# Six slots later: the loads of the context and of its transpose for the output side

## The chip, the cores and the metric

The kernel runs on one core of a Trainium2 chip. The metric is device time in microseconds of one launch, the median of a few runs. Engines are named as in the profile: PE is TensorE (PEld its weight loads), DVE is VectorE, ACT is ScalarE, POOL is GpSimd, SP is SyncE. SP and ACT also issue DMAs; their queues appear as SPq and ACTq.

## The reference

Two cross-attention layers over a batch of four, all in float32. Inputs are x (4, 256, 256) and a context (4, 512, 256).

```
# layer 0
q, k, v = LN(x) @ q_w + q_b, ctx @ k_w + k_b, ctx @ v_w + v_b      # 16 heads of 16
out     = softmax(q k^T / 4 + mask) v                               # 256 x 512 per head
hid     = out @ cproj_w + cproj_b + x
x1      = hid + gelu(LN(hid) @ fc_w + fc_b) @ proj_w + proj_b       # inner width 1024
# layer 1, one head of width 256
q, k, v = x1 @ w_q^T, ctx @ w_k^T, ctx @ w_v^T
result  = x1 + alpha * softmax(q k^T / 16) v @ w_o^T
```

## The kernel before

All matrix products are of float32 numbers that are split into a high and a low part (`_h`, `_l`; ScalarE makes the high part, VectorE or GpSimd the low one), three products for one.

**Slots.** Time is cut by hand into slots. A batch b has four groups of four heads, and a group has 8 slots. In slot s of group g, TensorE computes one tile of scores for the exponentials (`exp_tile`, L693, two matmuls), ScalarE takes its exponential (`exp`, L1107), and in between TensorE computes the score tiles from which VectorE takes the row maxima for the group one ahead (`max_tile`, L672; L1411), and the products with the values of the group one behind (`pv`, L703). Iteration b covers slots 7 to 38 (`at` in the code), where slots 8 to 15 belong to group 1, 16 to 23 to group 2, 24 to 31 to group 3, and 32 to 38 already to group 0 of batch b + 1. Beside the attention of batch b each slot has steps of two other batches:

- `pre(b + 1, ...)`: layer norm, transpose, query, key and value projections of the next batch (`PRE_AT` slots 9, 10, 16 and 22, `V_AT` 36 and 38).
- `post(b - 1, ...)`: the output projection, the second layer norm, the GELU layers and all of layer 1 for the batch before (`POST_AT`, or `LATE_AT` for batch 2). Of these, `NT` (slot 8 or 9) needs the rows x in `h`, `CT0` and `CT1` (slots 22 and 25, late 27 and 30) need the transposed context in `pT_raw` (L1126), and `CX` (27, late 34) needs the context in `pcx` (L1173).

Each engine runs its own program in this order; engines wait for one another by semaphores. There are two engines that issue DMAs.

**SyncE** loads the inputs of the next batch (`load_pre`), and stacks: `stack_group(b, g)` copies queries and keys of a group, high and low parts, into `q_stack` and `k_stack` (on-chip to on-chip), so that one matmul makes all three products at once. For one group these are three transfers of 64 KB (L520), a mask row (L525) and three of 128 KB (L530), the low part of the keys (`kp_l`) last. There is room for three groups, so the stacking of group 3 of a batch is released at slot 8, when the exponentials of group 0 have been computed; the groups 0 and 1 of the next batch follow at slots 16 and 24, and group 2 at slot 32. Each is read first eight slots after that. Nothing is stacked for a batch after the last.

**ScalarE** issues `load_post(b - 1)` (L1246 to L1251) at the beginning of slot `LOAD_AT` = 8 of iterations 1 to 3: the rows into `h` (256 KB), the context into `pcx` (512 KB), and its transpose into `pT_raw` (512 KB). Before the first it waits for `h_free`, the store of the batch before. The stores come from ScalarE as well (L1256).

In slot 10, `pre(b + 1, U_Q)` on ScalarE writes the high part of the next batch's queries over `qp_h` (L1079). It waits for TensorE's product and, by `await_stacked(act, range(NG), b)`, for the stacking of all four groups of the present batch, whose last transfer is the low part of the keys of group 3. GpSimd's `mask_row_of` (slot 11, L1740) waits for the same.

Of the kernel before, what the change touches and what calls it, by code (L numbers as in the profile page):

```python
# [94 lines left out]

GELU_CUBE, GELU_TANH, GELU_Y, GELU_SPLIT = 1, 2, 3, 4

LOAD_AT = 8


MAX_TILES = ((0, 1), (2, 3), (4,), (5,), (6,), (7,), (), ())
# [32 lines left out]
def build(nc, x, ctx, mask, ln1_w, ln1_b, q_w, q_b, k_w, k_b, v_w, v_b, cproj_w, cproj_b, ln2_w, ln2_b,  # L134
          fc_w, fc_b, proj_w, proj_b, l1_q, l1_k, l1_v, l1_o, alpha, ctx_t, q_t, k_t, vectors, out):
    with ExitStack() as stack:
# [177 lines left out]
        def steps_at(b):  # L314
            return LATE_AT if b == B - 2 else POST_AT

        def pre_at(b):
            return EARLY_AT if b == 1 else PRE_AT
# [150 lines left out]
        def slots(b, last):  # L469

            for at in range(START, START + NS):
                ab = b + 1 if at >= NS else b
                yield at, ab, at % NS // SLOTS, at % SLOTS, not (last and at >= NS)
# [593 lines left out]
        def _(act):  # L1067
            def pre(b, n):
                if U_K <= n < U_V:
                    return  # L1070
                act.wait_ge(pre_full, pre_use(b, n))
                if n < U_Q:

                    act.activation(zT[0][:].rearrange("p c n -> p (c n)"), pre_bank(b, n), ACT.Copy).then_inc(pre_hi, 1)
                elif n == U_Q:

                    await_stacked(act, range(NG), b)
                    for c in range(DC):
                        a = act.activation(qp[0][:, c, :], pre_bank(b, n)[:, c * LQ:(c + 1) * LQ], ACT.Identity, bias=bq[:, c:c + 1])  # L1079
                    a.then_inc(qh_done, 1)  # L1080
                elif n >= U_V:
                    i = n - U_V
                    await_(act, pv_done, NG * b)
                    act.activation(vals[:, 2 * i:2 * i + 2, :, 0:HD],
                                   pre_bank(b, n).rearrange("p (t h d) -> p t h d", t=2, h=H), ACT.Copy).then_inc(pre_free, 1)

            def context_high(b, c):

                act.wait_ge(cx_in, 16 * (b + 1))
                await_(act, pre_full, PRE_USES * b)  # L1090
                act.activation(cT[0][:, c, :], cx[:, c, :], ACT.Copy).then_inc(ct_high, 1)
# [18 lines left out]
            def o_out(b, g):  # L1110
                act.wait_ge(pv_done, NG * b + g + 1)
                act.activation(oT[:, g, :], om[:, 0:LQ], ACT.Copy).then_inc(o_done, 1)
# [51 lines left out]
            def post_slot(b, at):  # L1164

                if is_f(b, at - GELU_SPLIT):
                    gelu_high(b, chunk_of(b, at - GELU_SPLIT))
                if at in steps_at(b):
                    post(b, steps_at(b)[at])
                if steps_at(b).get(at) == "CX":  # L1170

                    wait_context(act, b)
                    act.activation(pc[0][:], pcx[:], ACT.Copy).then_inc(cx_high, 1)  # L1173
                if is_f(b, at - GELU_TANH):
                    gelu_tanh(b, chunk_of(b, at - GELU_TANH))

            def post_slot_end(b, at):
                if steps_at(b).get(at - 1) in ("S0", "S1"):
                    exp1(b, int(steps_at(b)[at - 1][1]))
# [51 lines left out]
            def tail_slot(at):  # L1231
                for i in tail_chunks(at - GELU_SPLIT):
                    tail_y_high(i)
                for step in tail_steps(at):
                    tail(step)
                for i in tail_chunks(at - GELU_TANH):
                    tail_tanh(i)
                for step in tail_steps(at - 1):
                    if step in ("S0", "S1"):
                        tail_exp(int(step[1]))  # L1240

            def pre_slot_end(b, at):
                if pre_at(b).get(at - 1, 0) >= U_K:
                    key_high(b, pre_at(b)[at - 1] - U_K)

            def load_post(b):  # L1246

                act.wait_ge(h_free, 16 * (b + 1))
                act.dma_start(h[:], x[b].rearrange("(p t) d -> p t d", t=TQ)).then_inc(h_in, 16)
                act.dma_start(pcx[:], ctx[b].rearrange("(p k) d -> p k d", k=TK)).then_inc(pcx_in, 16)  # L1250
                act.dma_start(pT_raw[:], ctx_t[b].rearrange("(c p) n -> p c n", p=P)).then_inc(pT_in, 16)  # L1251

            def store(b):
                bank, count = post_use(b, W_DL)
                act.wait_ge(post_free[bank], count + 1)
                act.dma_start(out[b].rearrange("(p t) d -> p t d", t=TQ), h[:]).then_inc(h_free, 16)  # L1256

            def prepare(step):
                if step == "WA":
                    act.wait_ge(prep_ps, 1)  # L1260
                    act.activation(wa[0][:].rearrange("p c n -> p (c n)"), work_ps[:, work_bank("prep", 0, "WA"), :], ACT.Copy, scale=L1_SCALE)\
                       .then_inc(w_hi, 1)
                elif step == "WO":
                    act.wait_ge(prep_ps, 3)
                    act.activation(wo[0][:].rearrange("p c n -> p (c n)"), work_ps[:, work_bank("prep", 0, "WO"), :], ACT.Copy).then_inc(w_hi, 1)
                elif step == "WC":
                    act.wait_ge(wc_in, 16 * NG)
                    act.activation(wc[0][:], raw_c, ACT.Copy).then_inc(w_hi, 1)
                elif step[:2] == "WF":
                    k = int(step[2])  # L1270
                    act.wait_ge(wf_in, 16)
                    act.activation(wf[0][:, k, :], raw_f[:, k, :], ACT.Copy, scale=vecs[:, V_LN2W + k:V_LN2W + k + 1])\
                       .then_inc(w_hi, 1)
                elif step[:2] == "WP":
                    half = slice(int(step[2]) * FC // 2, (int(step[2]) + 1) * FC // 2)
                    act.wait_ge(wp_in, 16)
                    act.activation(wp[0][:, half, :], raw_p[:, half, :], ACT.Copy, scale=0.5).then_inc(w_hi, 1)
# [26 lines left out]
            def attend(b, g, s):  # L1304
                nb, ng = ahead(b, g)
                pb_, pg = behind(b, g)
                if s == O_AT and not (isinstance(pb_, int) and pb_ < 0):
                    o_out(pb_, pg)
                exp(b, g, s)
                if s == ROWS_AT and not (isinstance(nb, int) and nb == B):  # L1310
                    max_rows(nb, ng)

            def iteration(b, first, last):
                for at, ab, g, s, attends in slots(b, last):
                    if not first and at == LOAD_AT:
                        load_post(b - 1)
                    if not last and at in CT_AT:
                        context_high(b + 1, CT_AT[at])
                    if not last and at in pre_at(b + 1):
                        pre(b + 1, pre_at(b + 1)[at])  # L1320
                    if not last and at in V_AT:
                        pre(b + 1, U_V + V_AT[at])
                    if not first:
                        post_slot(b - 1, at)
                    elif at in PREP_AT:
                        prepare(PREP_AT[at])
                    if last:
                        tail_slot(at)
                    if attends:
                        attend(ab, g, s)  # L1330
                    elif s == 0:
                        o_out(b, NG - 1)
                    if not last:
                        pre_slot_end(b + 1, at)
                    if not first:
                        post_slot_end(b - 1, at)
                    if not first and steps_at(b - 1).get(at - 1) == "DL":
                        store(b - 1)

            def epilogue():  # L1340
                for at in range(START + NS, LAST_SLOT):
# [3 lines left out]
                    if steps_at(B - 2).get(at - 1) == "DL":  # L1345
                        store(B - 2)

            run(act, iteration, prologue, epilogue)


# [546 lines left out]
```

## Time and profile before

| | us |
|---|---|
| median of three runs | 310.41 (308.37, 310.41, 323.36) |
| the profiled execution's own time | 313.87 |
| its span, first to last instruction | 312.1 |
| mean granted TensorE clock | 0.973 |
| TensorE busy | 268.1 (86%) |
| VectorE busy | 212.4 (68%) |
| ScalarE busy | 176.6 (57%) |
| GpSimd busy | 89.3 (29%) |
| DMA queue of SyncE (q1) | 17.31 MB, 23.8% of 16 engines |
| DMA queue of ScalarE (q10) | 5.52 MB, 6.4% |
| `k_stack<-kp_l` in the chain that ended last | 8% of the span |

Times of a row count from the first instruction of the span. Busy is the time in which an engine has an instruction running; a wait is told by its idle time and by what released it. The chain that ended last is followed back from the last instruction to whatever released each step. In this execution iteration 1 has its slot 8 at about 91.5 us, iteration 2 at 160.7 and iteration 3 at 228.4.

### The profile page before, as it was taken

To read this page: it belongs to the slowest core of one execution; us is meant where nothing else is said; L and a number is where in the kernel's file an instruction comes from. 1 tells how busy PE (TensorE), PEld (TensorE's weight loads), DVE (VectorE), ACT (ScalarE), POOL (GpSimd) and SP (SyncE) were. 2 spreads that over 40 slices of the span, in tenths; PEclk is the share of its full clock that TensorE was granted. 3 is DMA by queue.
4 is the path that set the end of the run, shared out by engine and by line. 5 is a ranking of instruction groups with operands and counts; after the bars stand their busy time and mean duration, and the time that the engine had idled before them with its cause. 6 is when DMAs were issued, how large, how long until landed. Compare 5 with 4: busy or idle time off the path is not lost.

```text
span 312.1 us, 5297 instructions
## 1 busy us (share of the span) xinstructions
PE 268.1 (86%) x2012; PEld 214.4 (69%) x2012; DVE 212.4 (68%) x368; ACT 176.6 (57%) x329; POOL 89.3 (29%) x108
## 2 busy tenths in 40 slices
PE   0757878997998699898988799998999999898995
PEld 0644647794676588676876587775877798578974
DVE  6776685677589458965488498847478766366854
ACT  3221575668472485956371786765375777526622
POOL 5551011102022139530012257430031174344100
PEclk9989599999799799999999999999999999999999
DMA  6038847711359002111638030205055000000000
GB/s 211 1 97 159 225 90 224 188 54 27 79 135 207 13 28 51 46 34 58 130 104 175 2 75 4 79 0 110 11 192 81 3 0 2 0 0 2 2 34 34
DMA packets 16456, 23.16 MB, mean 74 GB/s; under 512 B 2528, under 2 KB 9184, under 8 KB 16416
## 3 DMA queue, kind: packets, MB, share of 16 engines
q1 hardware_dynamic: 13360, 17.31, 23.8%
q10 hardware_dynamic: 3072, 5.52, 6.4%
q8 instruction: 16, 0.26, 0.4%
q14 instruction: 8, 0.07, 0.1%
HBM read 12.07 MB, written 1.05 MB: 42 GB/s over the span
## 4 chain that ended last, share of the span: by engine, by line
PE 54%; DVE 13%; DMA 8%; ACT 8%; POOL 7%; issue 5%; SPq 3%; ACTq 0%; POOLq 0%; DVEq 0%
PE work_ps L621 11%; DMA k_stack<-kp_l 8%; PE s L672 7%; PE om L703 6%; PE s L693 6%; PE work_ps L625 5%; DVE neg_max L1411 5%; PE work_ps L608 4%; ACT probs L1107 2%; PE s L621 2%; PE om L679 2%; SPq L520 2%; POOL ft L1771 2%; POOL max_cols L1727 1%; DVE ft L1480 1%
## 5 line engine op out<-in xcount | busy, mean ns | idle before, releaser
L1411 DVE TENSOR_REDUCE neg_max<-s 128x1 f32<-128x512 f32 x128 | 83.7, 684 | 20.8 <-PE s L672 20.3
L1107 ACT ACTIVATE probs<-s 128x512 f32<-128x512 f32 x128 | 75.5, 599 | 29.2 <-PE s L693 28.7
L693 PE MATMUL s<-q_stack,k_stack 128*128 128x256 f32 x256 | 57.5, 308 | 6.2 <-ACT probs L1107 5.4
L672 PE MATMUL s<-k_stack,q_stack 96*128 96x512 f32 x128 | 53.8, 453 | 4.7 <-DVE neg_max L1411 4.2
L693 PEld LDWEIGHTS s<-q_stack,k_stack 128*128 128x128 f32 x256 | 44.6, 200 | 14.0 <-ACT probs L1107 8.0
L672 PEld LDWEIGHTS s<-k_stack,q_stack 96*128 96x128 f32 x128 | 24.0, 202 | 20.9 <-DVE neg_max L1411 12.5
L703 PE MATMUL om<-probs,vals 128*17 128x256 f32 x512 | 33.7, 382 | 0.0
L1727 POOL CAST max_cols<-neg_max 128x8 fp32r<-128x8 f32 x16 | 5.8, 363 | 96.3 <-DVE neg_max L1411 96.3
L1099 ACT ACTIVATE q_stack<-om 8x1024 fp32r<-8x1024 f32 x16 | 16.3, 1018 | 8.1 <-PE om L679 7.8
L703 PEld LDWEIGHTS om<-probs,vals 128*17 128x17 f32 x512 | 11.9, 96 | 10.7 <-issue 0.3
L1422 DVE TENSOR_TENSOR y_l<-work_ps,y_h 128x512 fp32r<-128x512 f32 x12 | 8.3, 690 | 13.2 <-ACT y_h L1121 13.2
L1121 ACT ACTIVATE y_h<-work_ps 128x512 fp32r<-128x512 f32 x12 | 7.1, 596 | 17.7 <-PE work_ps L625 14.2
L1776 POOL TENSOR_TENSOR y_l<-fx,y_h 128x512 fp32r<-128x512 f32 x9 | 12.5, 1392 | 10.7 <-ACT y_h L1161 10.7
L1480 DVE SCALAR_TENSOR_TENSOR ft<-ft,fx 128x512 f32<-128x512 f32 x9 | 9.5, 1051 | 8.2 <-POOL ft L1771 8.2
L1745 POOL TENSOR_TENSOR kp_l<-kp_l,kp_h 128x512 fp32r<-128x512 f32 x7 | 9.0, 1284 | 20.7 <-ACT kp_h L1095 20.7
L1771 POOL TENSOR_TENSOR ft<-fx 128x512 f32<-128x512 f32 x9 | 10.3, 1139 | 11.1 <-ACT fx L1135 11.1
L608 PE MATMUL work_ps<-wv_h,cT_h 128*128 128x256 f32 x32 | 9.9, 309 | 3.4 <-DVE wv_l L1496 3.3
L679 PE MATMUL om<-ident,max_cols 128*104 128x128 f32 x32 | 7.1, 306 | 6.6 <-POOL max_cols L1729 6.6
L621 PE MATMUL work_ps<-aT_h,wf_h 128*128 128x256 f32 x48 | 12.7, 294 | 0.0
L621 PE MATMUL work_ps<-aT_h,wf_l 128*128 128x256 f32 x48 | 12.5, 291 | 0.0
L1079 ACT ACTIVATE qp_h<-work_ps,bq 128x256 fp32r<-128x256 f32 x8 | 3.4, 470 | 15.7 <-DMA k_stack<-kp_l 11.1
L621 PE MATMUL work_ps<-wp_h,y_h 128*128 128x256 f32 x48 | 12.0, 283 | 0.0
(290 smaller groups left out, 670.4 us busy)
## 6 DMA issues: line engine op xcount, KB each, us to landing
k_stack<-kp_h SPq DMA_DIRECT2D x32, 128.0 KB
cx<-in_ctx_t_dram SPq DMA_DIRECT2D x4, 512.0 KB, 4.5
k_stack<-kp_l SPq DMA_DIRECT2D x16, 128.0 KB
q_stack<-qp_h SPq DMA_DIRECT2D x32, 64.0 KB
pcx<-in_ctx_dram ACTq DMA_DIRECT2D x3, 512.0 KB, 4.7
pT_raw<-in_ctx_t_dram ACTq DMA_DIRECT2D x3, 512.0 KB, 9.8
xz<-in_x_dram SPq DMA_DIRECT2D x5, 256.0 KB, 4.1
q_stack<-qp_l SPq DMA_DIRECT2D x16, 64.0 KB
```

Source lines behind the costliest of these rows:

```text
L608: mm = pe.matmul(o, wi(w[a], k), vi(v[c], k), start=start and k == 0 and i == 0, stop=stop and k == n - 1 and i == 2)
L621: pe.matmul(o, wi(w[a], k), vi(v[c], k), start=start and i == k == a == c == 0, stop=False)
L625: mm = pe.matmul(o, wi(w[late[0]], k), vi(v[late[1]], k), start=False, stop=stop and i == len(terms) - 1 and k == n - 1)
L672: pe.matmul(s1[:, s1_bank(b, SLOTS * g + s), :], q_stack[0:ROW_MAX, hd, chunk(t)], k_stack[0:ROW_MAX, hd, :], start=True, stop=True).then_ ...
L679: mm = pe.transpose(om_rows[0:ROWS, chunk(t)], max_cols[:, t, :].bitcast(F32), ident[:])
L693: mm = pe.matmul(s2[:, s2_bank(b, SLOTS * g + s), i * LQ:(i + 1) * LQ], k_stack[:, hd, chunk(k)], q_stack[:, hd, :], start=True, stop=True)
L703: mm = pe.matmul(om[32 * j:32 * j + VW, 0:LQ], vals[:, k, j * NG + g, :], probs[:, g % 2, j, k, :], start=k == 0, stop=k == TK - 1)
L1099: act.activation(q_stack[ROW_MAX:ROWS, slots_of(b, g), :], om_rows[ROW_MAX:ROWS, :].unsqueeze(1).to_broadcast([2 * GH, GH, LQ]), ACT.Copy) ...
L1107: act.activation(probs[:, g % 2, s // 2, k:k + 2, :], s2[:, s2_bank(b, SLOTS * g + s), :].rearrange("p (k n) -> p k n", k=2), ACT.Exp).the ...
L1411: dve.tensor_reduce(neg_max[:, g % 2, s % 2, s // 2:s // 2 + 1], s1[:, s1_bank(b, SLOTS * g + s), :], AX.X, ALU.max, negate=True).then_inc ...
L1480: dve.scalar_tensor_tensor(f, f, 1.0 / GELU_CUBIC, fx[i % 3], ALU.add, ALU.mult).then_inc(cube, 1)
L1771: pool.tensor_tensor(ft[i % 3], fx[i % 3], fx[i % 3], ALU.mult).then_inc(square, 1)
```

## The change

`load_post` is split in two. The rows are still loaded at slot 8, behind the wait for `h_free`. The context and its transpose are issued at the beginning of slot 14, by the same engine, into the same buffers, with the same semaphores.

```
--- before.py
+++ after.py
@@ -95,7 +95,7 @@
 
 GELU_CUBE, GELU_TANH, GELU_Y, GELU_SPLIT = 1, 2, 3, 4
 
-LOAD_AT = 8
+LOAD_AT, LOAD_CONTEXT_AT = 8, 14
 
 
 MAX_TILES = ((0, 1), (2, 3), (4,), (5,), (6,), (7,), (), ())
@@ -1243,10 +1243,13 @@
                 if pre_at(b).get(at - 1, 0) >= U_K:
                     key_high(b, pre_at(b)[at - 1] - U_K)
 
-            def load_post(b):
+            def load_rows(b):
 
                 act.wait_ge(h_free, 16 * (b + 1))
                 act.dma_start(h[:], x[b].rearrange("(p t) d -> p t d", t=TQ)).then_inc(h_in, 16)
+
+            def load_context(b):
+
                 act.dma_start(pcx[:], ctx[b].rearrange("(p k) d -> p k d", k=TK)).then_inc(pcx_in, 16)
                 act.dma_start(pT_raw[:], ctx_t[b].rearrange("(c p) n -> p c n", p=P)).then_inc(pT_in, 16)
 
@@ -1313,7 +1316,9 @@
             def iteration(b, first, last):
                 for at, ab, g, s, attends in slots(b, last):
                     if not first and at == LOAD_AT:
-                        load_post(b - 1)
+                        load_rows(b - 1)
+                    if not first and at == LOAD_CONTEXT_AT:
+                        load_context(b - 1)
                     if not last and at in CT_AT:
                         context_high(b + 1, CT_AT[at])
                     if not last and at in pre_at(b + 1):
```

## Rows read from the trace of the kernel before

**Rows 1.** Window, slots 8-16: length, engines' busy us, PEclk, DMA share, GB/s.

```profile
91.55:112.09 20.54, 16.07 (x119) 12.64 (x118) 12.97 (x30) 9.98 (x20) 4.26 (x6) 0.92 0.46 94
```

**Rows 2.** The chain that ended last: start us, duration us, what.

```profile
95.41 9.08 DMA k_stack<-kp_l
...
104.59 0.84 ACT qp_h L1079 x2
...
164.56 8.07 DMA k_stack<-kp_l
...
172.74 0.85 ACT qp_h L1079 x2
...
232.25 9.24 DMA k_stack<-kp_l
```

**Rows 3.** Waits of the whole span: us, times, longest us.

```profile
ACT qp_h L1079 <- DMA k_stack<-kp_l: 11.1, 2, 6.1
```

**Rows 4.** Line L530: who waited for it (us, times).

```profile
  PEld s L672: 0.3, 1
```

**Rows 5.** TensorE's timeline: start us, us, instruction [idle before <-releaser].

```profile
100.42 0.28 PE L608 MATMUL work_ps<-zT_h,wq_l 128*128 128x256 f32 x1
...
103.04 0.50 PE L672 MATMUL s<-k_stack,q_stack 96*128 96x512 f32 x1
...
105.97 0.58 PE L693 MATMUL s<-q_stack,k_stack 128*128 128x256 f32 x1 [2.43 <-ACT probs L1107]
...
169.65 0.28 PE L608 MATMUL work_ps<-zT_h,wq_l 128*128 128x256 f32 x1
...
174.12 0.50 PE L693 MATMUL s<-q_stack,k_stack 128*128 128x256 f32 x2 [1.36 <-ACT probs L1107]
...
175.09 0.51 PE L693 MATMUL s<-q_stack,k_stack 128*128 128x256 f32 x2 [0.24 <-ACT probs L1107]
```

**Rows 6.** Windows with stacking in flight, and after it (columns as rows 1).

```profile
98.00:100.80 2.80, 2.80 (x32) 2.23 (x24) 2.48 (x9) 0.48 (x1) 0.70 (x1) 1.00 1.06 103
...
119.50:120.80 1.30, 1.30 (x20) 0.54 (x19) 0.35 (x1) 0.99 (x4) 1.30 (x3) 1.00 0.74 82
...
120.80:122.00 1.20, 1.20 (x13) 1.15 (x10) 1.16 (x1) 0.43 (x1) 1.20 (x2) 1.00 0.00 0
```

**Rows 7.** SyncE's timeline: the last stacking transfer of group (2,0).

```profile
118.14 0.55 SPq L530 DMA_DIRECT2D k_stack<-kp_l  x1
```

**Rows 8.** DMA issues: KB each, median us to landing.

```profile
pT_raw<-in_ctx_t_dram ACTq DMA_DIRECT2D x3, 512.0 KB, 9.8
...
h<-in_x_dram ACTq DMA_DIRECT2D x3, 256.0 KB, 3.2
```

**Rows 9.** Windows of TensorE after its two waits (columns as rows 1).

```profile
105.97:109.40 3.43, 3.43 (x14) 3.17 (x15) 2.76 (x5) 2.30 (x5) 0.39 (x2) 0.50 0.00 0
...
105.97:110.16 4.19, 4.19 (x21) 3.93 (x22) 2.76 (x5) 2.47 (x6) 0.39 (x2) 0.59 0.00 0
...
174.12:177.66 3.54, 3.02 (x22) 2.51 (x22) 2.75 (x5) 2.82 (x7) 0.39 (x2) 1.00 0.00 0
```

**Rows 10.** ScalarE's timeline with its DMA queue (ACTq), slots 8 to 22.

```profile
91.88 0.63 ACT L1091 ACTIVATE cT_h<-cx 128x512 fp32r<-128x512 f32 x1
...
91.95 0.45 ACTq L1250 DMA_DIRECT2D pcx<-in_ctx_dram  x1
...
107.78 0.60 ACT L1107 ACTIVATE probs<-s 128x512 f32<-128x512 f32 x1
...
109.99 0.84 ACT L1135 ACTIVATE fx<-work_ps,bf 128x256 f32<-128x256 f32 x2 [1.62 <-PE work_ps L625]
...
127.13 0.63 ACT L1126 ACTIVATE pT_h<-pT_raw 128x512 fp32r<-128x512 f32 x1
...
177.00 0.84 ACT L1135 ACTIVATE fx<-work_ps,bf 128x256 f32<-128x256 f32 x2 [0.72 <-PE work_ps L625]
```

**Rows 11.** TensorE's timeline: first maximum tiles of group (2,0).

```profile
127.99 0.63 PE L672 MATMUL s<-k_stack,q_stack 96*128 96x512 f32 x2
```

More of the change, by code:

```diff
@@ L96 @@
 GELU_CUBE, GELU_TANH, GELU_Y, GELU_SPLIT = 1, 2, 3, 4
-LOAD_AT = 8
+LOAD_AT, LOAD_CONTEXT_AT = 8, 14
 MAX_TILES = ((0, 1), (2, 3), (4,), (5,), (6,), (7,), (), ())
@@ L1244, in pre_slot_end, with load_rows, load_context @@
                     key_high(b, pre_at(b)[at - 1] - U_K)
-            def load_post(b):
+            def load_rows(b):
                 act.wait_ge(h_free, 16 * (b + 1))
                 act.dma_start(h[:], x[b].rearrange("(p t) d -> p t d", t=TQ)).then_inc(h_in, 16)
+            def load_context(b):
                 act.dma_start(pcx[:], ctx[b].rearrange("(p k) d -> p k d", k=TK)).then_inc(pcx_in, 16)
@@ L1315, in iteration @@
                     if not first and at == LOAD_AT:
-                        load_post(b - 1)
+                        load_rows(b - 1)
+                    if not first and at == LOAD_CONTEXT_AT:
+                        load_context(b - 1)
                     if not last and at in CT_AT:
```

## The prediction

> **What bounds the kernel now.** I read the page's busy shares first: TensorE is busy for 268.1 of 312.1 us, so a microsecond saved elsewhere counts only where TensorE stands still for it. Then I read the stretch around the moved loads. From slot 8 to slot 16 of iteration 1 the kernel takes 20.54 us, in which TensorE is busy for 16.07, VectorE for 12.97 and ScalarE for 9.98 [rows 1]: no engine fills it, something is waited for. The chain of waits says what. In each of iterations 1 to 3 it runs through the last transfer that stacks the keys of group 3, 8.07 to 9.24 us long, and in iterations 1 and 2 from there straight into `qp_h` on ScalarE [rows 2]. That is the wait of `pre(b, U_Q)` for all four stacked groups (the next batch's queries overwrite what stacking reads). It costs ScalarE 11.1 us in two waits, the longest 6.1, so the other is 5.0 [rows 3]. In iteration 3 there is no next batch, and group 3's stacking is waited for only by TensorE, for 0.3 us [rows 4].
>
> Not all 11.1 us reach TensorE. Its timeline shows it waiting for the exponentials queued on ScalarE behind `qp_h`: 2.43 us before 105.97 in iteration 1, and 1.36 and 0.24 us in iteration 2 [rows 5]. Before that it had its own query product to finish, which `qp_h` needs too: the last matmul of it starts at 100.42 and takes 0.28, so it is done at 100.70, and in iteration 2 at 169.93 [rows 5].
>
> Why does the stacking take 9 us? ScalarE's queue has issued 256 + 512 + 512 KB at slot 8, just ahead of it. While they share the DMA engines, these are full (share 1.06) though they move only 103 GB/s at the end of it. The same stacking for group (2,0), with no load beside it, has 0.74 at 82 GB/s in its last part and nothing in flight after 120.80 [rows 6]. Its last transfer was issued at 118.14 [rows 7], so it takes at most 2.66 us.
>
> **The change, part by part.**
>
> Step 1, slot 8. The row load (256 KB) stays, and it is first in its queue as before. Two issues, together 1 MB a batch, leave the slot, in iterations 1, 2 and 3. The row load has landed after 3.2 us in the median [rows 8]; nothing here slows it. The last stacking transfer, issued at 95.41 and 164.56, should land after 2.66 us, at 98.07 and 167.22; the lower bound is that value, the upper bound today's 9.08 [rows 2, 7]. I take the lower one, because what would remain beside the stacking (256 KB issued about 4 us earlier, landed after 3.2) is nearest to the undisturbed case. Even at 5.29 us (100.70 less 95.41) it would be hidden by the query product.
>
> Step 2, the wait of ScalarE. What is late next is that product: `qp_h` can start at 100.70 instead of 104.59 (3.89 us sooner) and at 169.93 instead of 172.74 (2.81 sooner) [rows 2, 5]. These 6.70 us are a ceiling for ScalarE. Queued behind `qp_h` are the exponentials of slots 10 and 11 and `aT_h`; they move by the same amount. In iteration 1 TensorE would have been ready at 105.97 - 2.43 = 103.54, and the exponential that releases it at 105.97 moves by 3.89, to 102.1. So the 2.43 us go whole. In iteration 2 the 1.36 and 0.24 us are both smaller than the 2.81 and go too: 1.60.
>
> Step 3, TensorE's clock. Right after the 2.43 us wait, the granted clock is 0.50, that is 1.2 GHz, from 105.97 to 109.40 [rows 9]. After the 1.36 us wait of iteration 2 it stays at 1.00, that is 2.4 GHz. The same instructions take 4.19 us in the first case and 3.54 in the second [rows 9], the latter with the 0.24 us already counted: 4.19 - 3.30 = 0.89 us. I take it as a gain, since the wait before it goes; the lower bound is zero (in another execution the low stretch may not be there, or may fall elsewhere).
>
> Step 4, iteration 3: TensorE's wait of 0.3 us for group (3,3) goes [rows 4].
>
> Step 5, slot 14. ScalarE now issues there the two transfers. An issue of this kind takes 0.45 us on its queue; at slot 8 the activation `cT_h`, later in the program, starts at 91.88, before the issue at 91.95 is shown [rows 10], so an issue does not hold the arithmetic. The bounds are 0 and 2 x 0.45 x 3 = 2.7 us. In slot 14 ScalarE then idles for TensorE anyway, 1.62 us in iteration 1 and 0.72 in iteration 2 [rows 10]. I take 0. SyncE and POOL are not behind these issues in program order; what they share is the DMA engines.
>
> Step 6, the loads' new neighbours. Slot 14 begins on ScalarE at 107.78 + 0.60 = 108.38. The transposed context lands after 9.8 us today, with stacking beside it [rows 8]: by 118.2. Its first reader, `pT_h` in slot 22, starts at 127.13 [rows 10], 18.75 us after the issue; this hides it, some 9 us to spare. The stacking of group (b+1,0), from slot 16 on, may meet the tail of these loads. It is first read at 127.99 [rows 11], 9.85 us after its last issue at 118.14. Even 9.24, the longest seen, fits. Cost 0.
>
> Sum: 2.43 + 0.89 + 1.60 + 0.3 = 5.2 us. The profiled execution took 313.87 us (span 312.1 and 1.8 around it), so it would become 308.7. It lies 3.5 us above the median of the runs, 310.41. With the same saving the median becomes **305.2 us**, 1.7% less.
>
> **Rivals.**
>
> Rival 1, the stacking is slow by itself. Its tail before the change has small throughput with full engines, and 82 GB/s also without a load beside it [rows 6]. If it landed halfway, after some 6 us, `qp_h` would gain 3 us but TensorE perhaps 1.5 in all: 308.9. Against it: at the end of that quiet stacking nothing was in flight 2.66 us after the issue.
>
> Rival 2, the gain is taken back. TensorE, sooner by 3 us, could meet the chain of GELU steps over POOL and VectorE from slot 14 on. If half is lost, 2.6 us are gained: 307.8. For it: VectorE is busy for 12.97 of what would become some 17.2 us [rows 1], 75%. Against it: this chain starts with `fx`, which itself waits for TensorE, so it moves along [rows 10].
>
> Rival 3, slower: the collision moves to group (b+1,0). The moved megabyte would have to push its last landing past the first read, over 9.85 us after the issue; beyond it TensorE loses a microsecond for each, in iterations 1 and 2 alone (iteration 3 stacks nothing after slot 14). At 12.5 us the gain of 5.2 is eaten, at 15.5 the median is 316.6. Against it: the longest landing with all 1.25 MB issued just ahead is 9.24, and here the issue of 1 MB lies 118.14 - 108.38 = 9.8 us ahead.
>
> Rival 4, slower: the context comes too late. ScalarE would stand at `pT_h` if the load took more than the 18.75 us, three times over; from 20.5 us on the kernel loses. At 22.5 us the median is 316.4. Today's 9.8 speaks clearly against it. The Trainium skill (DMA: Bandwidth & Descriptors, Rules for kernel authors) advises the opposite of this edit, to issue a DMA early and wait for it late so that its fixed cost overlaps. By that rule the change gives nothing or a loss; the trace differs here, in that the early issue costs others more than the 9 us of spare lead are worth.
>
> That the edit does nothing can be left out: the issues stand in ScalarE's own order, behind six more slots of arithmetic.
>
> **Numbers.** Forecast case 0.75: gain from 1.6 us (no clock, issues at 2.7: 5.2 - 0.9 - 2.7) to 7.9 (the ceiling 6.70 + 0.89 + 0.3), 302.5 to 308.8. Rival 1 has 0.09, rival 2 0.09, rival 3 0.04, rival 4 0.01; 0.02 is left for more than the ceiling (VectorE, freed as well). A measurement of this kernel can tell about 2%, 6.2 us, from no change, so faster begins below 304.2. Of the forecast case about a third, 0.27, lies there: where the 6.70 us arrive nearly whole, or where the low clock cost more. With the 0.02 faster is 0.29. The rest of the case and rivals 1 and 2 are within 2%: 0.66. Rivals 3 and 4 give 0.05 for slower. The range 302.0 to 309.3 takes in the forecast case and most of rivals 1 and 2, with half a microsecond more on either side for a median of three that came out between 308.37 and 323.36.
>
> **What would show it.** Step 1: the last stacking transfer lands under 3.5 us after its issue in slot 8. Step 2: `qp_h` on ScalarE waits for TensorE's product, not for a DMA, at most 2.3 us; TensorE's wait for `probs` before the exponential tile of slot 12 is gone in both iterations; slots 8 to 16 of iteration 1 take about 17.2 us. Step 3: no stretch at 0.50 there. Step 5: no idle time of ScalarE after the issues that is longer than before. Step 6: `pT_h`, `pc_h` and the first maximum tile of group (b+1,0) wait for no DMA. The prediction is wrong if stacking still lands after 5.3 us, if `qp_h` is released by a DMA again, or if slots 16 to 32 grow by what slots 8 to 16 lose.

## The result, and the profile after

The changed kernel takes 307.17 us (median of 10 runs, 305.65 to 312.54); the kernel before, on the same chip, 313.84 us (10 runs, 308.37 to 323.36). The executions of the kernel before scatter widely; set against each other without the disturbed ones, the ratio is **0.9896, 95% interval [0.9853, 0.9938]**: the change makes the kernel faster by 1.0%, about 3.2 us. That is inside the 2% to which the prediction gave 0.66, and the interval leaves out both no change and the forecast 1.7%. The profiled execution took 306.86 us with a span of 305.1; that of the kernel before 313.87 and 312.1. So the two traces differ by 7.0 us, twice what the timed runs show. Both numbers have to be explained.

The last stacking transfer of group 3 and what waits for it come first. This is the changed kernel's list of what kept `qp_h` on ScalarE idle (line L1079, us, times), which answers to [rows 3]:

```profile
  PE work_ps L608: 5.8, 3
```

No DMA is in it any more; in the kernel before it was a DMA for 11.1 us. ScalarE's timeline shows the same place in iterations 1 and 2, answering to [rows 2], with the two issues now in slot 14:

```profile
100.64 0.84 ACT L1079 ACTIVATE qp_h<-work_ps,bq 128x256 fp32r<-128x256 f32 x2 [2.25 <-PE work_ps L608]
...
104.20 0.35 ACTq L1253 DMA_DIRECT2D pcx<-in_ctx_dram  x1
...
104.58 0.45 ACTq L1254 DMA_DIRECT2D pT_raw<-in_ctx_t_dram  x1
...
165.56 0.84 ACT L1079 ACTIVATE qp_h<-work_ps,bq 128x256 fp32r<-128x256 f32 x2 [2.25 <-PE work_ps L608]
```

`qp_h` starts 2.25 us after ScalarE has become idle, released by TensorE's query product. The windows (columns as rows 1) are slots 8 to 16 and 16 to 24 of iteration 1, slots 8 to 16 of iteration 2, and the part of the stacking's window in which the DMA engines were still full before:

```profile
91.45:107.72 16.27, 14.23 (x119) 11.27 (x118) 12.98 (x30) 9.98 (x20) 4.33 (x6) 1.00 0.40 108
107.72:123.80 16.08, 15.02 (x119) 12.39 (x118) 14.23 (x19) 12.01 (x25) 10.51 (x10) 1.00 0.20 50
156.33:172.62 16.29, 14.26 (x119) 11.29 (x118) 12.97 (x30) 10.18 (x20) 4.39 (x6) 1.00 0.40 105
98.00:100.60 2.60, 2.60 (x31) 2.04 (x24) 2.28 (x8) 0.39 (x1) 0.70 (x1) 1.00 0.04 6
```

Slots 8 to 16 took 20.54 us in iteration 1 [rows 1] and take 16.27. From 98.00 on the DMA engines are all but idle (0.04; nothing moves after 98.20), where they were full up to 100.80 [rows 6]. The last stacking transfer was issued at 95.30, so it landed within 2.9 us. For iteration 2 and the slots after, these are the windows of the kernel before that the next sentences need:

```profile
112.09:128.19 16.10, 15.05 (x119) 12.39 (x118) 14.25 (x19) 12.02 (x25) 10.52 (x10) 1.00 0.17 39
160.73:179.58 18.85, 14.94 (x119) 11.24 (x118) 13.45 (x30) 10.52 (x21) 4.24 (x6) 1.00 0.46 102
179.58:195.35 15.77, 15.05 (x119) 12.40 (x119) 14.00 (x19) 11.57 (x24) 10.52 (x10) 1.00 0.17 39
228.42:312.10 83.68, 75.52 (x604) 63.27 (x603) 53.84 (x99) 46.20 (x94) 23.97 (x23) 1.00 0.12 30
```

```profile
172.62:188.71 16.09, 15.03 (x119) 12.39 (x119) 14.24 (x19) 12.02 (x25) 10.51 (x10) 1.00 0.17 52
221.78:305.10 83.32, 75.23 (x604) 63.17 (x602) 53.74 (x99) 46.08 (x94) 24.01 (x23) 1.00 0.09 30
```

The trace pair adds up: 20.54 - 16.27 = 4.27 us in iteration 1, 18.85 - 16.29 = 2.56 in iteration 2, 83.68 - 83.32 = 0.36 from slot 8 of iteration 3 to the end, less 16.09 - 15.77 = 0.32 given back in slots 16 to 24 of iteration 2: 6.9 of the 7.0 us.

### The profile page after: what moved, and what is told of

It reads as the page before. It is cut to its first block, busy times and chain, and to the rows that moved or that the text cites. A ratio compares the mean times of both kernels' runs of the same rounds, so it can differ in the third digit from the quotient of the medians.

```text
span 305.1 us, 5297 instructions
## 1 busy us (share of the span) xinstructions
PE 265.0 (87%) x2012; PEld 212.8 (70%) x2012; DVE 212.1 (70%) x368; ACT 176.5 (58%) x329; POOL 89.6 (29%) x108
## 4 chain that ended last, share of the span: by engine, by line
PE 55%; DVE 13%; ACT 10%; POOL 10%; issue 8%; DMA 3%; POOLq 0%; ACTq 0%; DVEq 0%
PE work_ps L621 11%; PE om L703 7%; PE s L672 7%; PE s L693 6%; PE work_ps L625 5%; PE work_ps L608 4%; DVE neg_max L1416 4%; DMA h<-in_x_dram 3%; POOL ft L1776 2%; ACT probs L1107 2%; PE s L621 2%; ACT q_stack L1099 2%; DVE ft L1485 2%; PE om L679 2%; POOL h L1763 1%
## 5 line engine op out<-in xcount | busy, mean ns | idle before, releaser
L693 PE MATMUL s<-q_stack,k_stack 128*128 128x256 f32 x256 | 56.5, 304 | 2.2 <-ACT probs L1107 1.4
L679 PE MATMUL om<-ident,max_cols 128*104 128x128 f32 x32 | 7.1, 306 | 6.7 <-POOL max_cols L1734 6.7
L621 PE MATMUL work_ps<-aT_h,wf_h 128*128 128x256 f32 x48 | 12.0, 283 | 0.0
L621 PE MATMUL work_ps<-aT_h,wf_l 128*128 128x256 f32 x48 | 11.8, 280 | 0.0
L621 PE MATMUL work_ps<-wp_l,y_h 128*128 128x256 f32 x48 | 11.8, 280 | 0.0
```

The costliest lines, as they stand in the source:

```text
L621: pe.matmul(o, wi(w[a], k), vi(v[c], k), start=start and i == k == a == c == 0, stop=False)
L679: mm = pe.transpose(om_rows[0:ROWS, chunk(t)], max_cols[:, t, :].bitcast(F32), ident[:])
L693: mm = pe.matmul(s2[:, s2_bank(b, SLOTS * g + s), i * LQ:(i + 1) * LQ], k_stack[:, hd, chunk(k)], q_stack[:, hd, :], start=True, stop=True)
```

## The experiments

All ratios are to the kernel before, measured at the same time; the changed kernel stands at 0.9896, and measured again later at 0.9912.

**x1_before**: the kernel before, no edit.

> The kernel before once more, unchanged, for a second profiled execution and its spread. The first trace pair puts the change's gain at 7.0 us (313.87 to 306.86), the timed runs at about 1% (3.2 us). Theory V (the stall of ScalarE behind the stacking of group 3 differs from execution to execution): in an execution of 308 to 311 us the two waits of qp_h on a DMA are shorter than 6.1 and 5.0 us, together 6 to 9, and slots 8 to 16 of iterations 1 and 2 take 17 to 19 us each instead of 20.5 and 18.9. Theory C (the stall is the same each time, only TensorE's clock differs): waits of 11.1 us in sum as before, slots 8 to 16 of iteration 2 at 18.9, and the difference lies in stretches at 1.2 GHz. Ratio to the kernel before 1.00 within 0.5%.

Ratio 1.0015 [0.9962, 1.0069]. Its profiled execution has a span of 307.1 us instead of 312.1. Its waits (engine, line waited for, us in total, times, longest):

```profile
ACT qp_h L1079 <- DMA k_stack<-kp_l: 7.6, 2, 4.0
```

Its slots 8 to 16 of iterations 1 and 2, its issues of the last stacking transfer on SyncE's queue, and `qp_h` on ScalarE:

```profile
91.41:109.23 17.82, 14.97 (x119) 11.26 (x118) 13.43 (x30) 10.29 (x21) 4.18 (x6) 1.00 0.48 108
157.49:174.88 17.39, 14.87 (x119) 11.27 (x118) 13.42 (x30) 10.48 (x21) 4.54 (x6) 1.00 0.48 111
109.23:124.97 15.74, 15.03 (x119) 12.39 (x118) 13.97 (x19) 11.59 (x24) 10.52 (x10) 1.00 0.18 40
```

```profile
95.27 0.59 SPq L530 DMA_DIRECT2D k_stack<-kp_l  x1
...
161.32 0.61 SPq L530 DMA_DIRECT2D k_stack<-kp_l  x1
```

```profile
102.37 0.84 ACT L1079 ACTIVATE qp_h<-work_ps,bq 128x256 fp32r<-128x256 f32 x2 [4.01 <-DMA k_stack<-kp_l]
...
168.03 0.84 ACT L1079 ACTIVATE qp_h<-work_ps,bq 128x256 fp32r<-128x256 f32 x2 [3.59 <-DMA k_stack<-kp_l]
```

The same program had its last stacking transfer through after 102.37 - 95.27 = 7.10 us and 168.03 - 161.32 = 6.71, where the first trace had 9.18 and 8.18 (from `qp_h` and the issue in [rows 2]), and its slots 8 to 16 took 17.82 and 17.39 us. Theory V holds: the stall varies from one execution to the next. A part of theory C is true as well: the stretch at 1.2 GHz that followed the wait in the first trace [rows 9] is absent here. Against this execution, the changed kernel gains 17.82 - 16.27 = 1.55 and 17.39 - 16.29 = 1.10 us, and gives back 16.08 - 15.74 = 0.34 in slots 16 to 24 of iteration 1 and about as much in iteration 2: 2.0 us, the difference of the spans (307.1 - 305.1). This execution, 308.81 us, is one of the short ones of the kernel before.

**x7_before**: the same once more, one execution.

> The kernel before a third time, one look. Two executions so far have landings of the last stacking transfer of 9.1 and 8.1 us (313.87 us in all) and of 7.0 and 6.6 us (an execution about 5 us shorter). If the landing beside the megabyte varies, this one lies between 6 and 10 us, and its time follows: about 1 us of time for each of landing above 5.3 us in each of iterations 1 and 2, less some 1.5 us that TensorE has in hand, plus about 0.8 us for each stretch at 1.2 GHz more.

It took 321.33 us, with a span of 319.6 and a mean clock of 0.936. One iteration is like x1, the other like the first trace:

```profile
100.24:118.20 17.96, 14.94 (x119) 11.24 (x119) 13.46 (x30) 10.32 (x21) 4.46 (x6) 1.00 0.47 107
166.48:187.08 20.60, 15.95 (x119) 12.50 (x118) 12.97 (x30) 10.20 (x20) 4.39 (x6) 0.92 0.43 93
180.80:184.20 3.40, 3.09 (x13) 2.83 (x14) 3.07 (x6) 2.61 (x6) 0.19 (x1) 0.50 0.00 0
```

```profile
111.35 0.84 ACT L1079 ACTIVATE qp_h<-work_ps,bq 128x256 fp32r<-128x256 f32 x2 [4.13 <-DMA k_stack<-kp_l]
...
179.73 0.84 ACT L1079 ACTIVATE qp_h<-work_ps,bq 128x256 fp32r<-128x256 f32 x2 [6.27 <-DMA k_stack<-kp_l]
```

```profile
181.11 0.79 PE L693 MATMUL s<-q_stack,k_stack 128*128 128x256 f32 x2 [2.61 <-ACT probs L1107]
```

The transfers were issued at 104.11 and 170.32, so they landed by 7.2 and 9.4 us. In the second, TensorE waited 2.61 us, and the clock was granted at 0.50 (1.2 GHz) from 180.8 on, as after the 2.43 us wait of [rows 5]. The landings lie in the range that was expected, 6 to 10 us; the 1.5 us that TensorE was said to have in hand were not there (see the table further down). Its other stretches at 1.2 GHz, to which the low mean clock belongs, lie before 92 us and outside this study.

**x2_ghost**: the megabyte put back at slot 8 as loads that nobody reads.

```
     act.wait_ge(h_free, 16 * (b + 1)); ... h ...            # slot 8
+    act.dma_start(pcx[:], ctx[b]...).then_inc(ghost_in, 16)
+    act.dma_start(pT_raw[:], ctx_t[b]...).then_inc(ghost_in, 16)
 def load_context(b):                                        # slot 14
+    act.wait_ge(ghost_in, 32 * (b + 1))
```

> The changed kernel, with the megabyte of slot 8 put back as a load that nobody reads (the same data into the same buffers, loaded again at slot 14). It tells contention of the transfers from everything else that the edit moved. If the gain is that the stacking of group 3 is free of the megabyte: qp_h waits for the stacking again, 5 to 6 us an iteration, slots 8 to 16 of iterations 1 and 2 take 18.5 to 20.5 us, and the time goes back to that of the kernel before (ratio 0.995 to 1.005). If the gain came from ScalarE's queue or from the order of its work alone, the time stays at the changed kernel's, ratio 0.99.

Ratio 1.0046 [0.9994, 1.0099]: the whole gain is gone. The wait is back, and slots 8 to 16 of iteration 1 take 17.53 us, near the 17.82 of x1; those of iteration 2 take 19.02, 3.4 us of them at 1.2 GHz (in this kernel, lines lie one further down):

```profile
ACT qp_h L1080 <- DMA k_stack<-kp_l: 7.5, 2, 3.8
```

```profile
95.20:112.73 17.53, 14.93 (x119) 11.24 (x118) 13.40 (x30) 10.25 (x21) 4.46 (x6) 1.00 0.64 167
```

Against the changed kernel, slot 8 differs only in the two issues and their transfers. (Slot 14 has a wait for the unread loads in addition; nothing stands there: `fx` waits 0.75 us for TensorE, as in x1.) What releases `qp_h` is the stacking transfer, not anything on ScalarE's queue, so the megabyte in flight is the cause. That it acts by filling the DMA engines is read from their share, 1.06 before [rows 6] and 0.04 after. The longest wait is 3.8 us, not 5 to 6; that is the size of x1.

**x3_half**: only `pT_raw` moves.

```
 def load_rows(b):
     ...
+    act.dma_start(pcx[:], ctx[b]...).then_inc(pcx_in, 16)   # slot 8
```

> Half of the change: only the transpose (pT_raw, 512 KB) goes to slot 14, the context (pcx) stays at slot 8. If the delay of the stacking goes with the bytes ahead of it (768 instead of 1280 KB; 256 in the changed kernel), the last stacking transfer lands about 5.9 us after its issue (halfway between 2.7 and 9.1), that is about 0.6 us after the query product is done at 5.3: qp_h waits about 0.5 us for it beside its wait for TensorE, and nearly the whole gain is kept, ratio 0.990 to 0.993. If any megabyte-size transfer there costs the same, ratio 0.995 or more.

Ratio 0.9895 [0.9814, 0.9977]. In iteration 2 the stacking takes from 162.00 to 168.43, 6.4 us instead of the 5.9 expected, and slots 8 to 16 take 17.12 us, 0.83 more than the changed kernel:

```profile
168.43 0.84 ACT L1079 ACTIVATE qp_h<-work_ps,bq 128x256 fp32r<-128x256 f32 x2 [3.32 <-DMA k_stack<-kp_l]
```

In iteration 1 `qp_h` waits for the product, since the clock is at 0.50 from 97.0 to 100.4 there; the wait ahead of it is the one of 0.95 us for `aT_l` that the other executions have as well. The interval is too wide to tell half from whole; the trace says that the half leaves a part of the stall.

**x4_slot10** and **x5_slot20**: `LOAD_CONTEXT_AT` = 10 and 20 instead of 14.

> Both loads two slots later instead of six (slot 10). They are then issued at about 98.5 us in the time of the trace, when the stacking of group 3 (last issue 95.4, landed about 98.1) is through. If only this window counts, the kernel behaves as the changed one, ratio 0.99, slots 8 to 16 at 16.3 us. If the six slots matter for another reason (a load beside the query and key work of slots 10 to 13, or the tail of the stacking still in flight), it is slower than the changed one by 0.3% or more and qp_h waits for a DMA.

> The changed kernel with both loads at slot 20, two slots before CT0 reads the transpose. Two slots are about 4 us (slots 16 to 24 take 16.1), and the transpose lands 4.2 us after its issue when nothing is beside it, but the stacking of group (b+1,0) and the copies of slot 17 to 19 are near. If the margin of 18.75 us (now some 17) was spare, as forecast, the cost is at most the part of the landing that sticks out: 0 to 2 us in iterations 1 and 2, a wait of pT_h for a DMA, none in iteration 3 where CT0 is at slot 27; ratio 0.988 to 1.000. If a late issue cost more than its landing (rule: issue early), the time is above the kernel before, over 1.005.

Ratios 0.9913 [0.9868, 0.9959] and 0.9905 [0.9853, 0.9957], both as the changed kernel, and slots 8 to 16 of iteration 1 likewise:

```profile
90.22:106.48 16.26, 14.21 (x119) 11.24 (x119) 12.95 (x30) 9.94 (x20) 4.01 (x6) 1.00 0.45 118
```

```profile
91.44:107.71 16.27, 14.23 (x119) 11.27 (x118) 12.98 (x30) 9.97 (x20) 4.34 (x6) 1.00 0.22 54
```

Even at slot 20, nobody waits for the context. The landings of the transpose there, and in the changed kernel (us, min/median/max):

```profile
DMA to landing us min/median/max: 4.2/4.5/5.0
```

```profile
DMA to landing us min/median/max: 4.1/4.2/4.4
```

So all three places that were tried, slots 10, 14 and 20, are as good: only the window of the stacking, about 91.5 to 98 us, has to be avoided. In x4 the loads are issued at 96.59 us, 2.5 us after the last stacking transfer (94.08), and from 96.6 to 97.5 us the DMA engines are idle (0.02): the stacking was just through. One of the twelve executions of x4 took 628.38 us; what happened there is not known, and the ratio leaves it out. The transpose, 9.8 us on its way before [rows 8], needs 4.2 with only the context ahead of it. The collision harmed both sides.

**x6_rows7**: `LOAD_AT` = 7, the rows one slot earlier.

> The changed kernel with the rows one slot earlier (slot 7). The chain that ended last now runs through the row load in iteration 3 and POOL waits 5.3 us for it there. If that wait decides, the row add, layer norm and transpose move up by up to 2 us and 1 to 3 us are gained (ratio 0.980 to 0.987). If the row add only has to be ready before the output projection is (in iteration 1 POOL is through with it at 96.3 and VectorE adds at 97.6), nothing is gained: ratio 0.989 to 0.992, as the changed kernel. I expect the second.

Ratio 0.9917 [0.9885, 0.9948]. GpSimd's wait for the rows falls from 12.0 to 7.4 us and nothing is gained: that wait is not what ends last.

**x11_more**: 1.5 MB of unread loads at slot 8, as x2 with one load more.

```
+    act.dma_start(fx2[:]..., ctx[b]...).then_inc(ghost_in, 16)
```

> The changed kernel with 1.5 MB of loads that nobody reads issued behind the rows at slot 8 (the megabyte of the kernel before and 512 KB more, the context into another free buffer). How does the delay of the stacking go with the bytes ahead of it? If it queues behind them (in proportion), its last transfer lands 2 us later than with the megabyte, 8.7 to 9.3 us after the issue where no clock or other disturbance adds to it, and slots 8 to 16 of iterations 1 and 2 take some 19.5 us, ratio 1.010 to 1.018. If the two queues take turns, so that the stacking is slowed only while it is itself in flight, the added bytes come after it and cost nothing: 6.6 to 7.1 us, ratio 1.000 to 1.006.

Ratio 1.0193 [1.0121, 1.0265], clear of the 1.0046 [0.9994, 1.0099] of x2: the added bytes cost. The landings, 8.8 us both times, are those of the first guess; the stretches (20.4 and 20.0 us instead of 19.5) and the ratio came out above it. `qp_h`, and TensorE behind it, in iteration 1 (issue of the last transfer at 95.61, so 8.8 us):

```profile
104.43 0.84 ACT L1080 ACTIVATE qp_h<-work_ps,bq 128x256 fp32r<-128x256 f32 x2 [5.69 <-DMA k_stack<-kp_l]
```

```profile
105.80 0.50 PE L694 MATMUL s<-q_stack,k_stack 128*128 128x256 f32 x2 [2.01 <-ACT probs L1108]
...
174.79 0.80 PE L694 MATMUL s<-q_stack,k_stack 128*128 128x256 f32 x2 [1.99 <-ACT probs L1108]
```

```profile
91.75:112.18 20.43, 16.17 (x119) 12.63 (x119) 12.98 (x30) 9.97 (x20) 4.10 (x6) 0.92 0.61 171
160.81:180.84 20.03, 15.99 (x119) 12.56 (x118) 12.97 (x30) 10.20 (x20) 4.17 (x6) 0.91 0.63 174
106.40:109.80 3.40, 3.19 (x15) 3.02 (x15) 2.16 (x4) 1.68 (x4) 0.39 (x2) 0.50 0.34 106
174.60:178.00 3.40, 3.21 (x13) 2.95 (x14) 2.95 (x6) 2.50 (x6) 0.29 (x2) 0.50 0.06 12
```

Against x1, 512 KB more cost 1.7 to 2.1 us of landing. Against the first trace (9.2 and 8.2) they cost nothing that can be seen: the landings alone scatter too much, and it is the timed runs that tell. In both iterations TensorE's wait is about 2 us, and in both the clock stands at 1.2 GHz for 3.4 us, from within 0.6 us of the end of the wait.

**x9_after**: the changed kernel again.

> The changed kernel once more, on the same chip as the next two. Its slots 8 to 16 should again take 16.3 us in iterations 1 and 2, whatever the whole execution takes, because no transfer decides them any more; ratio to the kernel before 0.985 to 0.993.

Ratio 0.9912 [0.9868, 0.9955]; slots 8 to 16 take 107.75 - 91.46 = 16.29 and 172.63 - 156.37 = 16.26 us.

These runs and those of the result hold ten executions of the changed kernel with a mean clock of 0.978; they take 306.79 to 307.22 us. The kernel before has twenty with 0.977 or 0.978 among those that x1 to x11 were compared with; they take 307.90 to 311.75. So at one and the same clock the kernel before scatters over 3.9 us and the changed one over 0.4: the scatter went with the wait. It is the stall that differs, as between the first trace and x1.

**x8_low_later** and **x10_low14**: the changed kernel with VectorE's low halves of the next context later.

```
-CT_LOW_AT = {8: 0, 9: 1}
+CT_LOW_AT = {11: 0, 13: 1}      # x8;  x10: {11: 0, 14: 1}
```

> The changed kernel with one more step moved: VectorE makes the low half of the next batch's context (cT_l, two instructions of 0.68 us) in slots 11 and 13 instead of 8 and 9. In the changed kernel VectorE is full from 91 to 100 us, and TensorE waits there 0.69 us for neg_max and about 0.95 us for aT_l, each right behind a cT_l. If VectorE is what bounds slots 8 to 10 now that the stacking is out of the way, each wait shrinks by about 0.6 us: 1.2 us in each of iterations 1 and 2 (and perhaps 0), ratio 0.980 to 0.985. If another wait stands behind it, the ratio stays at 0.99.

> The changed kernel with VectorE's two low halves of the next context in slots 11 and 14 instead of 8 and 9. With slots 11 and 13 TensorE's waits near 94 and 96 us shrank by 1.1 us but it then waited 0.59 us for the row maxima at 105.0, behind the second cT_l in slot 13; VectorE idles 1.8 us in slot 14. If that place is the fault, slots 8 to 16 take 15.5 us instead of 16.1 in iterations 1 and 2 and the ratio is 0.980 to 0.985; if the waits only move on, it stays near 0.987.

Ratios 0.9865 [0.9819, 0.9912] and 0.9854 [0.9793, 0.9915]. The intervals overlap that of the changed kernel. At equal mean clock the executions part them: at 0.977 or 0.978, x8 takes 305.63 and 305.94 us and x10 305.28 and 305.62, where the changed kernel takes 306.79 to 307.22; at 0.982 or 0.983 they take 304.0 to 304.3, where it takes 305.6. The profiled execution of x8 has a span of 303.9 us against 305.1; that of x10 has 305.5, with a longer stretch at 1.2 GHz near 80 us. TensorE's timeline in x8 (the 0.69 us wait near 94 is gone, that for `aT_l` is 0.57 instead of 0.95, and a new one stands at 105):

```profile
94.48 0.36 PE L621 MATMUL work_ps<-wc_h,aT_h 128*128 128x256 f32 x1 [0.57 <-DVE aT_l L1427]
...
105.00 0.43 PE L679 MATMUL om<-ident,max_cols 128*104 128x128 f32 x2 [0.59 <-POOL max_cols L1734]
```

```profile
91.01:107.11 16.10, 14.45 (x119) 11.28 (x118) 13.55 (x30) 10.36 (x21) 4.01 (x6) 1.00 0.43 120
107.11:122.87 15.76, 15.04 (x119) 12.39 (x119) 13.93 (x18) 11.52 (x24) 10.52 (x10) 1.00 0.14 40
```

Of the 1.1 us won at 94 to 96 only 0.17 are left at slot 16 (16.10 against 16.27), and 0.32 more come in slots 16 to 24. In x10 slots 8 to 16 of iteration 1 take 15.90 us, and those of iteration 2 take 16.08, not 15.5: the waits only move on for the most part. These are the shortest times of the study, 1.4 and 1.5% below the kernel before.

## Why the prediction was right or wrong

The place, the cause and the direction were right; the size was not. 5.2 us (1.7%) were forecast, and 305.2 us where 307.17 were measured; 1.0% came in the timed runs, and 7.0 us between the two profiled executions. Two things were off, in opposite directions, so that the measured time lies in the stated range partly by luck. The terms of the sum (us), beside what each came to between the changed kernel and two executions of the kernel before:

| term | forecast | first trace | x1 |
|---|---|---|---|
| iteration 1, slots 8 to 16 (steps 2 and 3) | 2.43 + 0.89 | 4.27 | 1.55 |
| iteration 2, slots 8 to 16 (step 2) | 1.60 | 2.56 | 1.10 |
| from slot 8 of iteration 3 on (step 4) | 0.3 | 0.36 | 0.07 |
| slots 16 to 24, iteration 1 (step 6) | 0 | 0.02 | -0.34 |
| slots 16 to 24, iteration 2 (step 6) | 0 | -0.32 | -0.34 |
| sum | 5.2 | 6.9 | 2.0 |

**Step 1, the size of the stall: wrong for a usual execution.** "The last stacking transfer ... should land after 2.66 us" instead of 9.08: that it lands early is true (within 2.9 us in the changed kernel, within 2.5 in x4). But the 9.1 and 8.1 us of the one trace were taken as the kernel's value. Four more landings of the same program are 7.1 and 6.7 (x1), 7.2 and 9.4 us (x7). Of the executions around 308 to 311 us, on which the ratio rests, x1 is the one that was profiled: 7.1 and 6.7. At its clock it is among the short ones (308.81, where fifteen others on its chip have a median of 309.89), so the usual stall costs about 1 us more than in x1, and 2.0 + 1.1 us is near the 3.2 of the ratio. The text had noted that the profiled execution lay 3.5 us above the median, and then subtracted the same saving from either. That is the step that failed: the terms 2.43, 1.60, 0.89 and 0.3 are waits of one long execution, taken off the median. The extra 3.5 us and the saving were in part the same microseconds. In x1 the four terms, 5.2 us together, came to 1.55 + 1.10 + 0.07 = 2.7, of which 0.7 were given back in slots 16 to 24.

**Step 2, what TensorE gets: too small for the trace it was worked out from, and by the wrong path.** I gave TensorE only its waits for ScalarE, 2.43 and 1.60 us. Set side by side, the landings (from issue to `qp_h`), slots 8 to 16, and the time from the start of `qp_h` to TensorE's next transposes of the row maxima (`om`, L679) read:

| execution, iteration | landing | slots 8 to 16 | `qp_h` to `om` |
|---|---|---|---|
| after, 1 and 2 | `qp_h` at 5.3 to 5.4, set by the product | 16.27, 16.29 | 5.01, 5.00 |
| x3, 2 | 6.43 | 17.12 | 4.73 |
| x1, 2 | 6.71 | 17.39 | 4.74 |
| x2, 1 | 6.86 | 17.53 | 4.74 |
| x1, 1 | 7.10 | 17.82 | 4.74 |
| x7, 1 | 7.24 | 17.96 | 4.74 |
| before, 2 | 8.18 | 18.85 | 4.73 |
| x2, 2 (clock low ahead of the product) | 8.33 | 19.02 | 4.74 |
| x11, 2 and 1, with low clock | 8.79, 8.82 | 20.03, 20.43 | 5.35, 5.69 |
| before, 1, with low clock | 9.18 | 20.54 | 5.44 |
| x7, 2, with low clock | 9.41 | 20.60 | 5.28 |

From 6.43 to 8.18 us the stretch grows by 1.73 for 1.75: one for one, beginning at about 5.6. The last column says why. In all seven cases with a stall and a high clock, TensorE reaches these transposes 4.73 to 4.74 us after the start of `qp_h`, whatever the stall was. The path between the two runs through VectorE, not through the exponentials, and it stood in the chain that ended last of the trace of the kernel before (iteration 2), just below the rows that the prediction took from it:

```profile
172.74 0.85 ACT qp_h L1079 x2
...
173.61 0.88 DVE qp_l L1400 x2
174.49 0.60 DVE neg_max L1411
175.08 0.60 DVE aT_l L1422
175.68 1.21 DVE neg_max L1411 x2
...
177.22 0.21 POOL max_cols L1729
```

VectorE stands at `qp_l` (L1400) until `qp_h` is written (it needs the high part to make the low one). Behind it in VectorE's order are `aT_l` and three row maxima, and once the last of these is there GpSimd makes `max_cols`, for which the transposes wait. TensorE's timeline, before (iteration 2) and after (iteration 1):

```profile
177.47 0.42 PE L679 MATMUL om<-ident,max_cols 128*104 128x128 f32 x2 [0.27 <-POOL max_cols L1729]
```

```profile
105.65 0.38 PE L679 MATMUL om<-ident,max_cols 128*104 128x128 f32 x2
```

After the change TensorE no longer waits there and comes 5.01 us after `qp_h` (100.64): it has 0.27 us in hand, which is why the line begins at 5.6 and not at 5.3 to 5.4. The waits of 2.43 and 1.60 us for `probs` are only what TensorE loses on the way; the rest shows as shorter gaps up to the transposes. So the ceiling of step 2 less 0.27 us each, about 3.6 and 2.6 us (9.18 and 8.18 less 5.6), was the value to take for the profiled pair, not the 4.03 of waits. It is also what the changed kernel's slots 8 to 16 tell, 16.27 us where the prediction expected about 17.2. In x1 it is 1.55 + 1.10.

**Step 3, the clock: right for the first trace, not for the median.** In four cases TensorE waited 2.0 to 2.6 us there (2.43, 2.61, 2.01, 1.99), and each time the clock was at 0.50 afterwards; after waits of 0.2 to 1.4 us (before 2, x1, x2, x7 1) it was not. In the table the four lie 0.5 to 0.9 us above the line of the others (16.28 plus the landing less 5.6), beside the 0.89 of the sum. (The 3.30 us that this was reckoned from were themselves stretched by the stall: after the change the same instructions take 105.78 - 103.29 = 2.49 us. That part belongs to step 2.) But it belongs to the long stalls; x1 has none of it there. Four out of four does not make the wait its cause by itself: in x2 (from 165.5) and x3 (from 97.0) the clock fell to 0.50 for 3.4 us just behind TensorE's wait of 0.95 us for `aT_l`, a wait that in the other executions left it at 1.00.

**Step 4** was right for the first trace (0.36 us from iteration 3 on, 0.3 forecast) and worth nothing in x1, where TensorE does not wait for the stacking in iteration 3 and the same part takes 83.39 us against 83.32. **Step 5** was right: ScalarE's activation `oT` starts at 104.22, between the two issues at 104.20 and 104.58, so they do not hold the arithmetic there.

**Step 6**: no reader waits for the moved loads, as x5 shows at a far later place. The stacking of group (b+1,0) is not read late either. Yet slots 16 to 24 grew from 15.74 to 16.08 us against x1. Both values occur in the kernel before, 16.10 in iteration 1 of the first trace and 15.77 in iteration 2; the changed kernel has the longer one in both. This is rival 2 in small: at the end of the GELU chain TensorE waits 1.06 us for the row maxima in the changed kernel and 0.71 in x1. It is not the loads' doing, since it stays 16.08 with the loads at slot 20, and it goes with x8 (15.76), where VectorE's work lies otherwise. What orders it exactly was not tried.

**Rival 1** is refuted: the last stacking transfer landed within 2.9 us, not after some 6. **Rival 3** has no sign: in the changed kernel TensorE waits for no stacking at slot 24. **Rival 4** did not come true: the loads at slots 10, 14 and 20 all gain the same 1%, and nobody waits for them. The Trainium skill (DMA: Bandwidth & Descriptors, Rules for kernel authors) says to issue a DMA early and to wait for it late, because the fixed setup cost then overlaps. The runs do not contradict that reason, since even at slot 20 the loads land before they are read; what the prediction drew from it, no gain or a loss, was wrong. Here an early issue was paid for by another transfer that was needed sooner.

What stays open: why the same transfers, behind the same megabyte, land in 6.7 us one time and in 9.4 another; and why half the megabyte (x3) already makes it 6.4 us, nearly the 6.7 to 7.2 of the short cases with the whole.

## What to carry to other kernels

A small transfer that an engine will block on should not be issued just behind a large one that is needed much later; where the large one goes instead matters little, as long as it misses that window. Before a saving is read from a trace, compare the trace's own time with the median of the runs: if it lies above, the very wait that is to be removed may be what makes it long, and the saving must be taken at the wait's usual length. And when an instruction is held up, look at everything that waits for it, not only at the busiest engine's first wait: here the longer path to TensorE went through VectorE, which worked its list off in order behind the late `qp_l`.

## What the runs showed of the hardware

A stacking of some 600 KB, issued behind loads of another queue, had its last transfer landed 6.4 us after the issue with 768 KB ahead, 6.7 to 9.4 us with 1280 KB, 8.8 us with 1792 KB, and at most 2.9 us with 256 KB (issued at 95.30, nothing in flight from 98.20 on). The landings with 1280 and 1792 KB overlap; that the added bytes cost shows in the times (ratios 1.0046 and 1.0193 for x2 and x11). The scatter of 2.7 us between executions of one program, at the same bytes, was not expected. Nor was it that TensorE's clock fell to 1.2 GHz for 3.4 us in each of the four cases in which it had stood idle for 1.99 us or more at this place, and after none of the shorter waits for `probs` (0.2 to 1.36 us). A wait of 0.95 us a little earlier was followed by such a fall in two executions (x2, x3) and not in the others, so the length of one wait does not decide it.
